# An attention and feed-forward block in f32r: SBUF buffers laid out so that all matmul operands start at one byte of a 512-byte piece

## What is computed

```python
# cross attention on a layer-normed x, with its residual
q = (layernorm(x) @ Wq).reshape(B, Nq, 8, 64)
k = (context @ Wk).reshape(B, 77, 8, 64)
v = (context @ Wv).reshape(B, 77, 8, 64)
attn = softmax(einsum('bihd,bjhd->bhij', q, k) * 64 ** -0.5)
x = x + einsum('bhij,bjhd->bihd', attn, v).reshape(B, Nq, 512) @ Wo + bo
# feed-forward with weights stored as integers and scales for each 128 rows
h = layernorm(x) * gamma + beta
y = silu(h @ dequant(fc1_q, fc1_scales) + fc1_bias)      # 256 -> 1024
x = x + 0.5 * (y @ dequant(fc2_q, fc2_scales) + fc2_bias)  # 1024 -> 256
```

## Time and profile before

| | |
|---|---|
| median of 3 runs | 201.87 us (201.49 to 201.95) |
| profiled execution, own time | 201.96 us |
| its span, first to last instruction | 200.2 us |
| granted TensorE clock, mean | 1.000 |
| PE busy | 187.3 us (94%) |
| weight load busy | 180.1 us (90%) |
| DVE, ACT, POOL busy | 122.9, 121.9, 109.6 us |

### The profile page before, as it was taken

The page is one execution under the profiler, slowest core; times in us unless marked ns, Lnnn a source line. Parts: engine busy times, 40 slices in busy tenths (PEclk is TensorE's granted clock), DMA queues, the critical chain, the costliest instruction groups (busy, mean ns, idle before and its releaser), DMA issues.

```text
span 200.2 us, 3855 instructions
## 1 busy us (share of the span) xinstructions
PE 187.3 (94%) x1502; PEld 180.1 (90%) x1502; DVE 122.9 (61%) x262; ACT 121.9 (61%) x227; POOL 109.6 (55%) x135
## 2 busy tenths in 40 slices
PE   6989879789889999999999999999999998998994
PEld 6979669689878999899989999999999998998894
DVE  0487985899859544954495558746683577532341
ACT  2267960499708981787268934894289626754480
POOL 5034993269951957096708861695249544367020
DMA  6999950000000000000000000000000000000101
GB/s 164 318 403 368 260 166 5 2 0 3 0 27 1 29 0 0 29 26 0 3 26 26 3 0 28 29 2 0 26 29 0 3 0 28 28 0 3 49 3 52
DMA packets 9480, 10.72 MB, mean 54 GB/s; under 512 B 2268, under 2 KB 8183, under 8 KB 9335
## 3 DMA queue, kind: packets, MB, share of 16 engines
q1 hardware_dynamic: 8837, 9.70, 14.8%
q10 hardware_dynamic: 626, 0.79, 1.4%
HBM read 8.38 MB, written 2.10 MB: 52 GB/s over the span
## 4 chain that ended last, share of the span: by engine, by line
PE 51%; POOL 18%; DVE 12%; SPq 12%; issue 3%; DMA 1%; ACT 1%; DVEq 0%; ACTq 0%
PE H L785 18%; PE T L773 13%; PE T L797 10%; POOL y_lo L280 5%; SPq L213 4%; SPq L207 4%; PE S L752 4%; PE S L759 3%; POOL x_sb L274 3%; POOL rstd L262 3%; PE S L706 2%; DVE probs L524 2%; DVE smax L522 2%; POOL res_scale L266 2%; DMA vw_lo<-bo_lo 1%
## 5 line engine op out<-in xcount | busy, mean ns | idle before, releaser
L252 POOL TENSOR_TENSOR probs<-probs,rsum 128x616 f32<-128x616 f32 x16 | 19.1, 1217 | 39.9 <-DVE rsum L533 39.9
L280 POOL TENSOR_TENSOR y_lo<-y,y_hi 128x512 fp32r<-128x512 f32 x28 | 37.8, 1362 | 4.9 <-ACT y_hi L394 4.3
L785 PE MATMUL H<-hT_hi,w_hi 128*128 128x256 f32 x128 | 36.8, 288 | 2.2 <-issue 1.8
L797 PE MATMUL T<-w_hi,y_hi 128*128 128x256 f32 x128 | 37.0, 289 | 1.1 <-POOL y_lo L280 0.5
L363 ACT ACTIVATE probs<-probs,rstd 128x616 f32<-128x616 f32 x16 | 12.9, 808 | 40.4 <-DVE probs L524 40.4
L797 PE MATMUL T<-w_hi,y_lo 128*128 128x256 f32 x128 | 35.7, 279 | 0.0
L797 PE MATMUL T<-w_lo,y_hi 128*128 128x256 f32 x128 | 35.7, 279 | 0.0
L785 PE MATMUL H<-hT_hi,w_lo 128*128 128x256 f32 x128 | 35.5, 278 | 0.0
L785 PE MATMUL H<-hT_lo,w_hi 128*128 128x256 f32 x128 | 35.5, 277 | 0.0
L390 ACT ACTIVATE y<-H,vec 128x256 f32<-128x256 f32 x64 | 26.6, 468 | 8.4 <-PE H L785 8.4
L785 PEld LDWEIGHTS H<-hT_hi,w_hi 128*128 128x128 f32 x128 | 24.0, 188 | 3.8 <-issue 2.2
(11 more groups left out here) (115 smaller groups left out, 442.8 us busy)
## 6 DMA issues: line engine op xcount, KB each, us to landing
q_sb<-in_L_ffn_fc_q SPq DMA_DIRECT2D x2, 1024.0 KB, 13.2
out_x<-x_sb SPq DMA_DIRECT2D x16, 128.0 KB, 1.7
x_sb<-in_x SPq DMA_DIRECT2D x7, 256.0 KB, 5.6
s_sb<-in_L_ffn_fc_scales SPq DMA_DIRECT2D x2, 512.0 KB, 11.8
s_sb<-in_L_ffn_fc_scales SPq DMA_DIRECT2D x1, 1024.0 KB, 17.7
wq_sb<-in_L_xattn_Wq SPq DMA_DIRECT2D x1, 512.0 KB, 6.0
wo_sb<-in_L_xattn_Wo SPq DMA_DIRECT2D x1, 512.0 KB, 8.6
wk_sb<-in_L_xattn_Wk ACTq DMA_DIRECT2D x1, 384.0 KB, 4.5
```

The lines of the kernel that those rows point to most:

```text
L252: nc.gpsimd.tensor_tensor(p, p, rsum[:, j, :].unsqueeze(2).to_broadcast([P, HEADS, J]), ALU.mult).then_inc(norm_done, 1)
L280: nc.gpsimd.tensor_tensor(y_lo[:, two, :], y[:, two, :], f32(y_hi[:, two, :]), ALU.subtract).then_inc(y_lo_done, 1)
L785: ins = mm(r[:, q * W:(q + 1) * W], wt[:, c, m * P:(m + 1) * P], ht[:, c, :], start=i == 0, stop=i == len(steps) - 1)
L797: ins = mm(o, yt[:, m, j * P:(j + 1) * P], wt[:, m, :], start=m == 0 and i == 0, stop=m == M - 1 and i == 2)
```

## The change

It changes the order of declaration and pads two buffers, so that buffers that hold operands of f32r matmuls start at equal distances. The large buffers come first, all with sizes that are multiples of 512 bytes; the small ones (statistics, biases) come behind them through a new `small`, which counts their bytes, and a filler `rest_of_line` brings the following buffers (`y_hi`, `y_lo` and the early ones that share their space) back to the same byte. The half of M is padded from 308 to 384 columns, 1,536 bytes; the matmul still streams 308. The first byte of each operand within its 512-byte piece, from the declared sizes:

| operand | before | after |
|---|---|---|
| `w1_hi`, `w1_lo` (weights of fc1) | 192 | 128 |
| `hT_hi`, `hT_lo` (streamed in fc1) | 128 | 128 |
| `y_hi`, `y_lo` (weights of fc2) | 128 | 128 |
| `w2_hi`, `w2_lo` (streamed in fc2) | 192 | 128 |
| `pT_hi`, `pT_lo` (weights of attention_out) | 352 | 128 |
| `vw_hi`, `vw_lo` (streamed in attention_out) | 448 | 128 |
| `xT_hi`, `xT_lo` (weights of scores) | 160 | 128 |
| `m_hi`, `m_lo` (streamed in scores) | 16 different, among them 0, 16, 96, 128, 192, 304 and 432 | 128 |
| `ident`, `probs`, `x_sb`, `hn` (f32 transposes) | 448, 160, 128, 128 | 128 |

All starts are multiples of 16 bytes before and after.

```diff
@@ build_program
+    HALF_COLS = -(-HALF * 4 // LINE) * LINE // 4
...
+        used = 0
+
+        def small(name, shape):
+            nonlocal used
+            used += -(-math.prod(shape[1:]) * 4 // GRAIN) * GRAIN
+            return sb(name, shape)
+
         x_sb = sb("x_sb", [P, NT, D])
-        bo_sb = sb("bo_sb", [1, D])
-        bo_hi, bo_lo = sb("bo_hi", [1, D], F32R), sb("bo_lo", [1, D], F32R)
-        vec = sb("vec", [P, 2 * C + M])
...
-        m_hi, m_lo = sb("m_hi", [P, B, C, 2, HALF], F32R), sb("m_lo", [P, B, C, 2, HALF], F32R)
+        m_hi, m_lo = sb("m_hi", [P, B, C, 2, HALF_COLS], F32R), sb("m_lo", [P, B, C, 2, HALF_COLS], F32R)
         vw_hi, vw_lo = sb("vw_hi", [P, B * JC, D], F32R), sb("vw_lo", [P, B * JC, D], F32R)
+        xT_hi, xT_lo = sb("xT_hi", [P, C, W], F32R), sb("xT_lo", [P, C, W], F32R)
+        pT_hi, pT_lo = sb("pT_hi", [P, UT, JC, P], F32R), sb("pT_lo", [P, UT, JC, P], F32R)
+        hT_hi, hT_lo = sb("hT_hi", [P, C, W], F32R), sb("hT_lo", [P, C, W], F32R)
...
+        vec = small("vec", [P, 2 * C + M])
...
+        sb("rest_of_line", [P, (-used % LINE) // 4])
@@ m_heads
-            return m[:, b, n // 2, :, :].rearrange("p h (k e j) -> p (h k) e j", k=K // 2, e=2)[:, :, n % 2, :]
+            return m[:, b, n // 2, :, 0:HALF].rearrange("p h (k e j) -> p h k e j", k=K // 2, e=2)[:, :, :, n % 2, :]
@@ m_lo_part
-                    nc.vector.scalar_tensor_tensor(m_heads(m_lo, b, n), ps[bank][:, 0:HALF].rearrange("p (k j) -> p k j", k=K), DH ** -0.5 / D,
-                                                   f32(m_heads(m_hi, b, n)), ALU.mult, ALU.subtract).then_inc(freed[bank], 1)
+                    r = ps[bank][:, 0:HALF].rearrange("p (h k j) -> p h k j", h=2, k=K // 2)
+                    for h in range(2):
+                        ins = nc.vector.scalar_tensor_tensor(m_heads(m_lo, b, n)[:, h, :, :], r[:, h, :, :], DH ** -0.5 / D,
+                                                             f32(m_heads(m_hi, b, n)[:, h, :, :]), ALU.mult, ALU.subtract)
+                    ins.then_inc(freed[bank], 1)
@@ scores
-                            ins = mm(o, xt[:, c, j * P:(j + 1) * P], m[:, b, c, h, :], start=n == 0, stop=n == len(steps) - 1)
+                            ins = mm(o, xt[:, c, j * P:(j + 1) * P], m[:, b, c, h, 0:HALF], start=n == 0, stop=n == len(steps) - 1)
```

More of the change, by code:

```diff
@@ L1 @@
+import math
 from contextlib import ExitStack
@@ L19 @@
 UT = 2
+LINE = 512
+GRAIN = 32
 def build_program(nc, x, ctx_in, wq, wk, wv, wo, bo, gamma, beta, q1, s1, b1, q2, s2, b2, out):
@@ L80, in sem @@
             return stack.enter_context(nc.semaphore(name))
-        x_sb = sb("x_sb", [P, NT, D])
-        bo_sb = sb("bo_sb", [1, D])
-        bo_hi, bo_lo = sb("bo_hi", [1, D], F32R), sb("bo_lo", [1, D], F32R)
-        vec = sb("vec", [P, 2 * C + M])
-        gamma_sb, beta_sb, b1_sb = vec[:, 0:C], vec[:, C:2 * C], vec[:, 2 * C:2 * C + M]
-        b2_half = sb("b2_half", [P, D])
+        used = 0
[3 more added lines that the diff above has]
+            return sb(name, shape)
+        x_sb = sb("x_sb", [P, NT, D])
         q1_sb = sb("q1_sb", [P, C, F], I32)
@@ L94, in build_program @@
         w2_hi, w2_lo = sb("w2_hi", [P, M, D], F32R), sb("w2_lo", [P, M, D], F32R)
-        m_hi, m_lo = sb("m_hi", [P, B, C, 2, HALF], F32R), sb("m_lo", [P, B, C, 2, HALF], F32R)
+        m_hi, m_lo = sb("m_hi", [P, B, C, 2, HALF_COLS], F32R), sb("m_lo", [P, B, C, 2, HALF_COLS], F32R)
         vw_hi, vw_lo = sb("vw_hi", [P, B * JC, D], F32R), sb("vw_lo", [P, B * JC, D], F32R)
-        ident = sb("ident", [P, P])
-        neg_half = sb("neg_half", [P, NT])
-        table_probe = sb("table_probe", [P, 1])
@@ new lines, in build_program @@
+        hT_hi, hT_lo = sb("hT_hi", [P, C, W], F32R), sb("hT_lo", [P, C, W], F32R)
+        hT = sb("hT", [P, C, W])
+        hn = sb("hn", [P, UT, D])
+        y = sb("y", [P, M, W])
+        probs = sb("probs", [P, UT, JC * P])
+        ident = sb("ident", [P, P])
+        bo_sb = sb("bo_sb", [1, D])
+        bo_hi, bo_lo = sb("bo_hi", [1, D], F32R), sb("bo_lo", [1, D], F32R)
+        b2_half = sb("b2_half", [P, D])
+        vec = small("vec", [P, 2 * C + M])
+        gamma_sb, beta_sb, b1_sb = vec[:, 0:C], vec[:, C:2 * C], vec[:, 2 * C:2 * C + M]
@@ new lines, in build_program @@
+        neg_half = small("neg_half", [P, NT])
+        table_probe = small("table_probe", [P, 1])
+        bn1, mv1 = small("bn1", [P, NT, 6]), small("mv1", [P, NT, 2])
+        veps1, rstd1 = small("veps1", [P, NT]), small("rstd1", [P, NT])
+        smax, ssum, rsum = small("smax", [P, UT, HEADS]), small("ssum", [P, UT, HEADS]), small("rsum", [P, UT, HEADS])
+        bn2, mv2 = small("bn2", [P, 2, UT, 6]), small("mv2", [P, 2, UT, 2])
+        vars2, rstd2 = small("vars2", [P, 2, 2, UT]), small("rstd2", [P, 2, 2, UT])
@@ L119, in build_program @@
+        neg_rstd2, res_scale, res_shift = small("neg_rstd2", [P, 2, UT]), small("res_scale", [P, 2, UT]), small("res_shift", [P, 2, UT])
+        sb("rest_of_line", [P, (-used % LINE) // 4])
         early = ExitStack()
@@ L345, in m_hi_part @@
                     r = wait_filled(act, f"M{b}.{n}")
-                    nc.scalar.activation(m_heads(m_hi, b, n), r[:, 0:HALF].rearrange("p (k j) -> p k j", k=K), ACT.Copy,
+                    nc.scalar.activation(m_heads(m_hi, b, n), r[:, 0:HALF].rearrange("p (h k j) -> p h k j", h=2, k=K // 2), ACT.Copy,
                                          scale=DH ** -0.5 / D).then_inc(m_hi_done, 1)
```

## The result

The changed kernel takes 203.30 us (median of 9 runs, 202.63 to 204.07) against 201.91 us for the kernel before (9 runs). The ratio is 1.0069, with a 95% interval of 1.0049 to 1.0088. I had forecast 199.5 us. The sign was wrong and the time lies outside the range.

The account below looks back on a forecast made before the run. PE was taken to bound the kernel only where the chain of waits runs through it. Gains of 1.27 us in five rounds, 0.31 ahead and 0.79 in the last pairs, 2.4 in all, gave 199.5 us; range 197.6 to 202.6.

Parts of the forecast that it names:

- The bound and the chain: A steady round of 20.84 us shortens only by gains in fc1, attention_out and 18 fc2 matmuls; the rest is shadowed.
- What a matmul costs today: On PE: fc1 114 ns, fc2 118, attention_out 120, scores 141 between starts, with the clock full in the whole span.
- Does the layout cause this?: Whether operand start bytes set PE's paces: two readings spoke against it, one left it open.
- The first reading: fc2 and fc1 each run at two paces, 113.5 or 114 and 118 ns, with the same addresses.
- The second: Scores run at 141 to 142 ns whatever the streamed operand's start, so that start, alone or against the weights, makes no difference.
- What is left is the start of the weights: Weights 32 bytes off a multiple of 64 go with 13 ns excess, so attention_out and scores should come down.
- The padding and the rest: Splitting m_lo on DVE costs 0.15 us each, 1.2 us for eight, hidden behind the bias row; other parts cost 0.
- my own sign: If the first attention_out starts later than 28.95 us, the split m_lo was not hidden.
- The sum: All kinds at fc1's pace: attention_out gains 6 ns, fc2 4, scores 5.4, last fc1 4; in all 2.4 us; chance 0.34.
- slower: Rival: streams starting at one byte interfere, fc1 and fc2 go to 120 ns, 203.7 us; chance 0.14.
- 0.24 us against 0.18: In the slower rival, per nanosecond over the rounds: fc1 costs 0.24 us, attention_out and 18 of fc2 give back 0.18.
- The full rate: Rival: equal starts bring f32r matmuls to 109 ns and scores to 131, 5.9 us gained, 196.0 us; chance 0.13.

Follow-up runs that it names:

- the old bytes: The changed kernel, with its buffer order, padded M and sixteen m_lo instructions, but every f32r operand at its byte in the kernel before; median 201.57 us, ratio 0.9996.
- the kernel with fc1 undone: The changed kernel with only the weights of fc1 back at 192, 64 bytes past the streamed operand; median 202.02 us, ratio 1.0022.

## Why the prediction was wrong

**The bound and the chain: right.** The round is what counts. The 0.27 us of fc1 and 0.02 us of fc2, less 0.08 us at the transposes, give the 0.21 us that the round grew by. The slower fc2 of tile 0 in the shadow cost nothing; it ate from PE's wait for DVE, as did most of the stretch at the lower clock.

**What a matmul costs today: right.** 114, 118, 120 and 141 ns stood in the rows, and the old bytes gave the same paces again, though not in the same stretches. The clock was not at full speed in the whole span: the `warm` matmuls at its start, 128 columns of f32, start 213 ns apart until 4.4 us, twice the 108 ns of the earlier trace rows. No term of the sum lies there.

**"Does the layout cause this?": the step that failed.** The first reading, two paces at one address, was sound, and it is what was seen at 64 bytes. The second was the mistake. I took scores, whose 24 matmuls ran at one pace whatever their bytes, as evidence that the distance makes no difference, and carried it over to the kinds with 256 columns. Scores heed it little, and the other way round: 24 of them took 3.60 us in the last pairs at distance 0, 3.66 at 64, and 3.63 in the kernel before. Equal starts are the slowest for 256 columns and among the fastest for 308. So what I saw in scores said nothing of fc1, whose 48 matmuls of a round went from 114 to 120 ns. Why 256 columns heed the distance more isn't shown. One could think that their stream of 107 ns is about as long as the load of the weights, and that of scores, 128 ns, longer. But no row gives the load: the f32 transposes, each with its own weights, start every 108 to 109 ns, and that can be their own stream, as f32 matmuls of 256 columns take 215 ns each (six in 1.29 us in the changed kernel). No kernel here has another number of columns.

**"What is left is the start of the weights": the conclusion that failed.** Both operands at 352 or both at 0 gave the same 120 ns. The multiple of 64 was a coincidence of four kinds with different distances.

**The padding and the rest: nothing on the chain, as forecast, at less than half of the price that I gave.** Two m_lo instructions before, and the four that stand in their place, on DVE (start us, us):

```profile
24.30 0.85 DVE L503 SCALAR_TENSOR_TENSOR m_lo<-H,m_hi 128x308 fp32r<-128x308 f32 x2
24.30 0.98 DVE L517 SCALAR_TENSOR_TENSOR m_lo<-H,m_hi 128x154 fp32r<-128x154 f32 x4
```

That is 0.13 us for two, 0.065 us each; I had estimated 0.15. The durations alone (469 ns before, 307 to 308 for a half) would say 0.147, but on DVE too one instruction starts before the duration of the last is over. It was hidden. By my own sign it was not, as the first attention_out started at 29.35 us and not at 28.95. The sign was a bad one: the last lo part of the probabilities was through on DVE at 28.03 us (27.92 before), and the bias row, whose transfer no m_lo holds up, landed at 29.10 (28.67 before).

**The sum and the rivals.** Each term of the sum had the gain of 4 to 6 ns that never came. The rival *slower* named the place (fc1 and fc2), the mechanism (both at one byte) and the pace (120). Its price was 203.7 us and the median is 203.3. It counted 6 ns for all 48 matmuls of a round, 0.29 us; the rows have 0.27, of which 0.08 came back at the transposes. I gave it 0.14, because of the evidence of scores. The comparison "0.24 us against 0.18" in it was worked out wrongly: 48 matmuls of attention_out and fc2 in each of five rounds give back 0.24 us a nanosecond too, as much as fc1 costs. The rival had the only positive evidence, that fc1 is fastest with a distance of 64, and I should have asked what would happen to the kind that was already good. *The full rate* never showed: no f32r stretch in any kernel was below 113 ns. The Trainium skill, "SBUF — State Buffer", section "Who interferes with whom", says that PE's two read ports are independent and that PE never waits on anyone. By that the layout should change nothing, and here the same matmuls take 114 or 120 ns by the distance of their operands; the measurement decides. What inside PE waits for what, no run shows. The Trainium skill, "TensorE: Matmul & The Clock Gate", section "Back-to-back issue gap", gives N / 2.4 + 2.5 ns for an isolated matmul, from which I estimate 109.2 ns for 256 columns; the section says itself that weight loads change this in a stream of matmuls, and no f32r stretch here comes down to it.

## What to carry to other kernels

A kind of work that already runs at the best pace is what a uniform layout can spoil, so before making all alike, ask which of the present cases is the fastest and try the others like that one. Evidence from one shape doesn't carry over to another when the two have different limits. For f32r matmuls of 256 columns on this chip, weights that begin 64 bytes past the streamed operand, counted within 256 bytes, were worth 0.6% in one layout, 0.45% in another and nothing that could be measured in a third, where M was not padded; equal starts were, beside 160 bytes, the slowest of eight distances.

## What the runs showed of the hardware

For f32r matmuls of 256 columns the pace follows the table of distances above, in which 256 bytes were as 0. And there is a lock: at equal starts, in the changed kernel, a stretch of fc1 or fc2 wanders, mostly between 116 and 121 ns, for up to eight starts and then stays at 120 until it ends; attention_out, right behind fc1, has 120 from its first.

The granted clock fell for a while in five of the profiled kernels, and not in the nine others. In the changed kernel it was at 0.65 of full in the mean of the stretch from 40.9 to 45.3 us, in fc1 of pair 0:

```profile
42.62 0.41 PE L800 MATMUL H<-hT_hi,w_hi 128*128 128x256 f32 x1
42.84 0.41 PE L800 MATMUL H<-hT_lo,w_hi 128*128 128x256 f32 x1
```

There the starts are 213 ns apart, which is the lower of the two levels, 1.2 GHz. What PE did before: it had stood idle 1.7 us for the bias row and again 1.78 us ahead of fc1. In the kernel with fc1 undone it came sooner. PE waited 2.3 us for the bias row, and this is the next row of its chain:

```profile
30.18 5.30 PE T L798 x30
```

30 matmuls took 5.30 us in place of 3.83, and they began 1.23 us later than in the kernel before, together 2.70 us. That execution took 204.83 us, 2.8 us above the median of its kernel. In the nine profiles with a mean clock of 0.999 and more the wait for the bias row was 1.6 us or less, in the five others 1.7 us or more. The wait goes with the bias row's transfer, which took 2.89 us from its issue in the kernel before and 3.70 here, though no kernel changed it, and with when PE gets there: with the old bytes the transfer took 3.28 us and PE waited 0.6. That the long wait makes the clock fall was not tested by an experiment. On the changed kernel it has little effect: its runs with the lower clock took 203.30 to 203.99 us, the others 202.63 to 204.07.
